# Token lists of the routed experts: the last group's by products of 0/1 matrices, the second group's scatters all in steps 29 and 30

## The reference

```python
K, V, Q = x @ theta_K.T, x @ theta_V.T, x @ theta_Q.T
for each token:                       # W, b carried along the sequence
    g = 2.0 / d_h * (W @ k + b - v)
    W = W - LR * outer(g, k); b = b - LR * g
    out = W @ q + b
x = layernorm(x + out)
shared = silu(x @ sW1 + sb1) @ sW2 + sb2
logits = x @ routing_W.T + expert_bias
top_vals, top_idx = top_k(sqrt(softplus(logits)), 2)      # 2 of 8 experts
y_e = silu(x @ rW1[e] + rb1[e]) @ rW2[e] + rb2[e]
x = layernorm(x + shared + sum over the token's 2 experts of top_val * y_e)
```

## Time and profile before

| | us |
|---|---|
| median of 3 runs | 2340.74 |
| profiled execution | 2332.68 |
| its span | 2330.9 |
| PE busy in the span | 2200.8 (94%) |
| PEld busy | 1905.5 (82%) |
| DVE busy | 1524.9 (65%) |
| POOL busy | 1218.7 (52%) |
| ACT busy | 916.8 (39%) |
| 128 scatters (L1793), first to last start | 902.8 to 1915.7 |

### The profile page before, as it was taken

One profiled execution on the slowest core, in us unless ns is written; L12 is line 12 of the kernel. 1 busy time (PEld: TensorE's weight loads), 2 busy tenths in 40 slices (PEclk: granted clock), 3 DMA queues, 4 the chain that ended last, 5 costly groups with the idle time before them and its releaser, 6 DMA issues.

```text
span 2330.9 us, 40319 instructions
## 1 busy us (share of the span) xinstructions
PE 2200.8 (94%) x12738; PEld 1905.5 (82%) x12738; DVE 1524.9 (65%) x3794; ACT 916.8 (39%) x2136; POOL 1218.7 (52%) x1168
## 2 busy tenths in 40 slices
PE   8999999999999999999999999997889789999896
PEld 6888888888888888888888888885778678888775
DVE  5666666666666776666666676664354336887798
ACT  4333333334334333433333433331444335544444
POOL 1345534445433336665455532465556565777667
PEclk9999999999999999999999999998899899999998
DMA  4212222111221111222111110008333225887896
GB/s 169 73 64 73 82 87 77 64 66 71 82 87 51 37 37 40 71 82 86 51 37 41 42 55 28 29 19 354 112 111 119 94 92 182 294 289 240 284 328 215
DMA packets 112203, 257.18 MB, mean 110 GB/s; under 512 B 21618, under 2 KB 23282, under 8 KB 109056
## 3 DMA queue, kind: packets, MB, share of 16 engines
q1 hardware_dynamic: 83776, 187.35, 22.9%
q0 software_dynamic: 27936, 67.22, 8.8%
q10 hardware_dynamic: 288, 0.04, 0.0%
HBM read 160.36 MB, written 105.26 MB: 114 GB/s over the span
## 4 chain that ended last, share of the span: by engine, by line
PE 47%; DVE 8%; issue 5%; ACT 2%; POOL 2%; another core or an unknown queue 1%; DMA 1%; DVEq 1%; SPq 0%; ACTq 0%; POOLq 0%
PE banks L114 14%; PE banks L116 14%; PE banks L115 13%; PE banks L763 2%; PE banks L120 2%; DVE b_Y L1138 1%; DVE b_XL L1135 1%; DVE b_small L1690 1%; PE banks L790 1%; DVE b_Y L1135 1%; DVE b_HL L1135 1%; POOL W L1747 1%; PE banks L505 1%; DVEq L1655 1%
## 5 line engine op out<-in xcount | busy, mean ns | idle before, releaser
L114 PE MATMUL banks<-W 128*128 128x512 f32 (+1 forms) x2040 | 743.3, 364 | 14.5 <-DVE W L1135 7.6
L116 PE MATMUL banks<-W 128*128 128x512 f32 (+1 forms) x2040 | 717.9, 352 | 0.0
L115 PE MATMUL banks<-W 128*128 128x512 f32 (+1 forms) x2040 | 717.6, 352 | 0.0
L114 PEld LDWEIGHTS banks<-W 128*128 128x128 f32 x2040 | 388.3, 190 | 59.7 <-DVE W L1135 7.5
L116 PEld LDWEIGHTS banks<-W 128*128 128x128 f32 x2040 | 387.1, 190 | 54.3
L115 PEld LDWEIGHTS banks<-W 128*128 128x128 f32 x2040 | 388.4, 190 | 42.4
L1747 POOL TENSOR_TENSOR W<-S,W 128x512 fp32r<-128x512 f32 (+1 forms) x249 | 321.0, 1315 | 137.8 <-ACT W L834 137.2
L834 ACT ACTIVATE W<-banks 128x512 fp32r<-128x512 f32 x320 | 189.8, 594 | 345.4 <-PE banks L116 140.1
L1747 POOL TENSOR_TENSOR X<-X,B 128x1024 f32<-128x1024 f32 x32 | 76.9, 2404 | 421.7 <-DMA X<-in_x 421.6
L834 ACT ACTIVATE W<-S 128x512 fp32r<-128x512 f32 (+1 forms) x256 | 161.8, 654 | 213.7 <-DVE S L1135 207.3
L1135 DVE TENSOR_TENSOR W<-banks,W 128x512 fp32r<-128x512 f32 x192 | 132.3, 689 | 152.2 <-ACT W L834 152.2
(11 more groups left out here) (171 smaller groups left out, 4434.8 us busy)
## 6 DMA issues: line engine op xcount, KB each, us to landing
RG<-ys SPq DMA_DIRECT2D x128, 256.0 KB
XT<-in_xT SPq DMA_DIRECT2D x32, 512.0 KB
X<-in_x SPq DMA_DIRECT2D x32, 512.0 KB
x1d<-X SPq DMA_DIRECT2D x64, 256.0 KB
wd<-RG SPq DMA_DIRECT2D x32, 512.0 KB, 3.9
W<-wd SPq DMA_DIRECT2D x16, 1024.0 KB, 13.1
out<-b_Y SPq DMA_DIRECT2D x64, 256.0 KB
zd<-X SPq DMA_DIRECT2D x52, 256.0 KB, 2.0
```

What stands on the lines that cost most here:

```text
L114: e.matmul(o, ll, rh, start=start, stop=False, skip_group_check=True)
L115: e.matmul(o, lh, rl, start=False, stop=False, skip_group_check=True)
L116: return e.matmul(o, lh, rh, start=False, stop=stop, skip_group_check=True)
```

## The change

The change has four parts.

1. Group 1's 24 tiles are scattered in steps 29 and 30, 12 tiles (24 scatters) each. From step 26 on nine scatters, not one, stand ahead of `xb`.
2. Group 2 has no scatters, no table in DRAM and no `load_ids`. Its routing ends in the slot (`rSL`) and the row in the slot (`rPP`) of each of the 24 (tile, choice) pairs. `lists` on DVE makes from them, for each pair, a 0/1 matrix of rows (`OH`, 128 x 128) and a 0/1 matrix of slots times the token's number in two parts (`rLR`, 128 x 62); `places` on PE sums their products in 24 matmuls after pass 50; `places` on DVE turns the sum into `IDX` in pass 52, where empty places keep the spare number loaded at the start.
3. What waited for the group's table (`tokens`, `send`, `rows`) now waits for the last step of that.
4. The memory for POOL's DMA descriptors is set to 8192 bytes per partition where the default was used.

```diff
-SCATTERS = [[3] * 10, [8, 8]]
+SCATTERS = [[3] * 10, [12, 12]]
...
-    p.scatter.update({36 + j: (c, c["tile"] + j // 2, j % 2) for j in range(2 * c["tiles"])})
...
+    def places(g):
+
+        o = bank(w, ("list", g["x"]), k.s_oh, one_hots(g) + 5)
+        w.wait_ge(k.s_oh, one_hots(g))
+        n = 2 * g["tiles"]
+        for m in range(n):
+            z = mm(e, o[:, 0:2 * g["slots"]], k.OH[:, m, :], k.rLR[:, m, :, :].rearrange("p y s -> p (y s)"), m == 0, m == n - 1)
+        z.then_inc(k.s_list, 1)
...
         if i == 20:
             count(last)
+        if i == 50:
+            places(last)
...
-        if i in (32, 66):
-            load_ids(k, e, w, k.groups[1 if i == 32 else 2])
+        if i == 32:
+            load_ids(k, e, w, k.groups[1])
...
+    def lists(g):
...
+        tt(hi, iotaS.unsqueeze(1).to_broadcast(full), k.rSL.unsqueeze(2).to_broadcast(full), ALU.is_equal).then_inc(k.s_oh, 1)
+        yield
+        w.wait_ge(k.s_oh, 1)
+        e.tensor_scalar(lo, hi, low, None, ALU.mult).then_inc(k.s_oh, 1)
+        yield
+        w.wait_ge(k.s_oh, 2)
+        tt(hi, hi, high.unsqueeze(2).to_broadcast(full), ALU.mult).then_inc(k.s_oh, 1)
+        yield
+        for m in range(0, n, 4):
+            y = min(4, n - m)
+            cells = [P, y, P]
+            tt(k.OH[:, m:m + y, :], iotaP.unsqueeze(1).to_broadcast(cells),
+               k.rPP[:, m:m + y].unsqueeze(2).to_broadcast(cells), ALU.is_equal).then_inc(k.s_oh, 1)
+            yield
+
+    def places(g):
...
+        w.wait_ge(k.s_list, 1)
+        w.wait_ge(k.d_zero, 48)
+        e.tensor_copy(a, o[:, 0:NS]).then_inc(k.s_oh, 1)
+        n = one_hots(g)
+        w.wait_ge(k.s_oh, n + 1)
+        e.tensor_scalar(b, a, 0.0, None, ALU.is_equal).then_inc(k.s_oh, 1)
+        stt(c, o[:, NS:2 * NS], float(P), a, ALU.mult, ALU.add).then_inc(k.s_oh, 1)
+        w.wait_ge(k.s_oh, n + 3)
+        stt(a, IDX, 1.0, b, ALU.add, ALU.mult).then_inc(k.s_oh, 1)
+        w.wait_ge(k.s_oh, n + 4)
+        stt(IDX, c, -1.0, a, ALU.add, ALU.add).then_inc(k.s_oh, 1)
...
-    routes = [route(last)]
+    routes = [route(last), lists(last)]
...
+        if i == 52:
+            places(last)
...
-        next(scattered, None)
+        for _ in range(9 if t >= k.groups[-1]["step"] else 1):
+            next(scattered, None)
         xb(t)
...
-    nc = _bacc.Bacc("TRN2", target_bir_lowering=False, num_devices=1)
+    nc = _bacc.Bacc("TRN2", target_bir_lowering=False, num_devices=1, dynamic_dma_scratch_size=8192)
```

65 lines of the change are left out of this document (54 added, 11 removed).

## The result

| | before | changed |
|---|---|---|
| median (4 runs each, taken side by side) | 2338.73 us | 2286.01 us |
| lowest to highest | 2336.39 to 2342.3 | 2283.8 to 2294.19 |
| profiled execution, its span | 2332.68, 2330.9 | 2283.8, 2282.0 |

The ratio is 0.977, with a 95% interval of 0.9751 to 0.9788: 52.7 us less by the medians, 48.9 by the profiled executions, where 62.0 were forecast. Later the same kernel was measured twice more beside the kernel before, on chips 8 and 13: 0.9762 (0.9739 to 0.9786) and 0.974 (0.9718 to 0.9762). On two other chips, 9 and 11, the kernel before itself takes about 2249 us, and there the halves and variants of the change that ran win 0.3% or less by their medians (the changed kernel itself didn't run there).

What follows compares the result with a forecast made beforehand. PE was taken to set stage two's pace at 3.5 us a pass, except where POOL's scatters held passes to about 5 us. Gains of -28.2 and -40.3 plus added terms of 2.5, 2.3, 1.2, 0.5: -62.0, 2279 us; range 2264 to 2295.

Steps and rivals of the forecast that it cites:

- term 7: Steps 29 and 30: eight more scatters each ahead of `xb`, hidden by POOL's idle time; 0, bounds 0 to 27 us.
- terms 1 and 2: Passes 2 to 17 and 36 to 59 lose 16 and 24 scatters, leaving 3.5 us a pass: -28.2 and -40.3 us.
- the four windows: Stage two, passes 20-24, 24-32, 32-36, 64-75: no scatters; PE said to set the pace, about 3.5 us a pass.
- Term 3: Passes 5 and 7: ACT's table changes, covered by stalls until now, come to light; +2.5 us (0 to 5.7).
- Term 4: PE's 24 new matmuls of 62 columns, priced by a bf16 weight load of 95 ns: +2.3 us.
- Term 5: Down product of slot 51 waits for PE's bank until DVE's five operations of pass 52 end: +1.2 us (0 to 2).
- Term 6: DVE's new list operations in place of routing steps, at most two in a pass: +0.5 us (0 to 3).
- the second rival: Scatters pile up in steps 29 and 30, `xb` late: +12.4 us, up to 27; 2291 to 2306 us; chance 10%.
- Only the queue of POOL: Stage two: only POOL's excess of 3.94 against 3.5 us a pass goes, lumps stay; -11.1, 2330 us; chance 7%.
- Descriptors run out of room: All 149 passes of stage two: POOL's DMAs wait for smaller descriptor memory; +111 us, 2452 us; chance 4%.
- No effect: Scatter passes take 5 us for another reason, only the added 6.5 us are seen; 2347 us; chance 2%.
- the signs of being wrong: ACT's remote waits stay without scatters; DVE waits for POOL in step 29 or 30; POOL's DMA rows exceed 1.05 us.

Runs made afterwards that it cites:

- filled_2: Changed kernel with a POOL product without DMA in each of passes 2 to 17 and 36 to 59, on chip 13; 2275.83 us, ratio 0.9752.
- combined: Changed kernel with POOL's stores and gathers (passes 6 to 61) tied to PE, scatters in steps 29 and 30 broken by waits, nine only from step 29; 2264.03 us, 0.9701.
- changed_3: The changed kernel unaltered, measured again beside the kernel before on chip 13; 2274.37 us, ratio 0.974.
- broken: Changed kernel, but every fourth scatter of steps 29 and 30 waits until the one just before has landed; chip 9, 2247.14 us, ratio 0.9985.
- runs_rows: Changed kernel with 5 to 13 extra POOL DMAs of 128 rows of 512 bytes ahead of `xb` in steps 5 to 13; chip 11, 2244.28 us.
- g1_only: Kernel before with only group 1's scatters moved into steps 29 and 30, group 2 scattered as before; chip 9, 2248.60 us, ratio 0.9999.

## Why the prediction was right, and where its sizes were off

**The mechanism** ("long unbroken runs of data DMAs on POOL delay the signals between the other engines") held, on chips of the first kind: filled_2 has POOL as busy and no remote wait while its products last, combined has all 13 scatters of step 30 without the delay, and where POOL's passes are tied to PE the waits are gone. That it depends on the chip could not be seen in one trace, and the prediction said nothing of it; that the result came from a chip like that of the trace was luck. The price is the 90 us by which the kernel before differs between chips, of which the change wins back some 50 and combined some 70.

**The step that failed** stands right behind it: "a kernel whose POOL has slack again doesn't make such runs". The changed kernel does. It makes one of eleven scatters in step 30 (term 7), and in stage two it makes runs of four for many passes after POOL has fallen behind once, though it has 0.84 us to spare in a pass (terms 1 and 2). The prediction gave 0 to both.

**Terms 1 and 2**, with what they bring to light: -25.7 and -36.3 forecast, -23.8 and -34.5 measured, and -24.7 and -37.2 in changed_3 beside the profile before. They are off by 2 us each only because two errors meet. The alternation costs 67.5 - 63.0 and 103.8 - 99.0, 4.5 and 4.8 us beside combined, which shows that the 3.5 a pass are to be had: the four windows from which they were taken had no such mode, and over a stretch with it a pass takes up to 3.77 on the mean (half of 7.54). Against it stand the terms below, of which most was not there. The last of the four windows was cut wrongly as well: 1972.60 is not a store. Eleven passes from 1934.17 end at 1975.62 and take 41.45 us, 3.8 each, since from pass 72 on a pass has more to do; up to there 8 passes take 27.96, and the 3.5 stand. The least that was put for both terms, POOL's own excess of 7.0 and 10.6 us, isn't borne out: on chip 9 the excess costs PE nothing.

**Term 3**, ACT's tables, +2.5: nothing. combined has both table changes in passes 5 and 7 and takes 63.04 us from pass 2 to 20, 18 x 3.50, and broken and runs_rows take 63.0; what the tables do is to start the alternation where signals are late. **Term 4**, PE's matmuls, +2.3: 0.9 measured. The weight load of 95 ns was the wrong row: the loads have 98 ns each here too, but overlap, so that the pairs stand 32 ns apart. The Trainium skill (TensorE: Matmul & The Clock Gate, Back-to-back issue gap) gives 81 ns for 128 columns; for these 62 columns the trace has less than half of that. **Term 5**, the bank wait, +1.2: 0.82. **Term 6**, DVE, +0.5: no wait of another engine for a step of `lists` was found, other than the longer stores of POOL below. Together terms 4 to 6 come to the 1.0 us by which passes 36 to 64 of combined are over 98.

**Term 7**, "The idle time of POOL hides them: 0", is where it cost most. For `xb` it was right, 3.8 us to spare in step 30. But the run was held against the add alone, and not against the very mechanism on which terms 1 and 2 rest. In the prediction that stood under the second rival ("if the runs of 9 and 13 delay signals too"), with 10%; up to the first store it made +9.4, 8.1 of it in step 30, and its own mechanism (`xb` late) did not occur. So a part of this rival came true beside the forecast, and they had been treated as excluding each other. With the 2 us each of the two windows and the +3.0 (alternation) and -2.6 behind pass 64 this makes the difference of 13 us between 48.9 and 62.0. By the medians it was 9.3. (The high end of the range, by the terms given for it, adds up to 2296 us and not to 2295.)

**Only the queue of POOL** was given 7%. It is right for chips 9 and 11 in that there are no lumps, and wrong even there in its price: POOL's 3.94 us a pass are caught up with later, and g1_only is as fast as the kernel before. Its rule, by the Trainium skill (SBUF — State Buffer, Who interferes with whom), that PE and ACT never wait on anyone, speaks of the ports of this memory. ACT's 3.52 us beside the run in step 30 are a wait for a signal; whether they have to do with memory no run here shows. **Descriptors run out of room**: no; the stores are 1.02 us and the gathers 1.03, but for those below. **No effect**: no.

**Of what would show it**: the clock, the end of the scatters (1610 us) and `xb` in time came; 1.15 us of idle came in part of the passes only. Of the signs of being wrong three came in part. The remote waits of ACT did not stay at 72.9 us, but 50.7 of them are left. The add of step 30 is 9.3 us later than before, without a wait for POOL. And the DMA rows grew over 1.05 us in one place, which is here, POOL's stores of passes 32 to 35 and DVE's `lists`:

```profile
1767.89 1.53 POOL L1992 DMA_INDIRECT ys<-b_Y,IDX  x1 [2.95 <-DVE b_Y L1164]
...
1774.09 1.39 POOL L1992 DMA_INDIRECT ys<-b_Y,IDX  x1 [0.31 <-issue]
```
```profile
1767.60 0.92 DVE L1164 TENSOR_TENSOR RG<-smallc,RG 128x744 bf16<-128x744 f32 x1
...
1773.89 1.29 DVE L1164 TENSOR_TENSOR OH<-smallc,RG 128x512 bf16<-128x512 f32 x2 [0.22 <-issue]
```

Each store that lies beside one of these operations, which read both operands from SBUF, takes 0.3 to 0.5 us longer. It cost nothing: PE was busy 13.09 of the 13.09 us of passes 32 to 36.

## What to carry to other kernels

Don't issue DMAs in an unbroken row from POOL while other engines work closely together: put an operation or a wait between them, or tie each to PE's progress. Four in a row were enough in stage two, and slack alone doesn't prevent them, since POOL makes such a row each time it catches up. A window cut by the rows of an engine that lags shows its lag and not the time of the kernel; take the same passes by the engine that sets the pace, or up to where the other has caught up. When a mechanism carries the gain of a change, hold every other part of the change against it too; here the scatters that were moved made in step 30 what they had ceased to make in stage two. And measure on more than one chip before a gain is believed: this one was worth 2.3 to 2.6% in three measurements, and on two other chips, where the changed kernel itself didn't run, its halves and variants gave 0.3% or less.
